# Graph network with two mixtures of experts: ranks by running counts, biases on VectorE, another order in the first router, five row buffers, small groups of tiles at both ends

## The chip, the cores and the metric

One Trainium2 chip, one of its cores. The kernel is one program; its metric is the time of an execution in microseconds (us) on the device, and a kernel's time is the median of its runs. TensorE (PE, with its weight loads PEld), VectorE (DVE), ScalarE (ACT), GpSimd (POOL) and SyncE (SP) run in parallel and wait for each other by semaphores. A granted clock of 1.0 is TensorE's upper level, 2.4 GHz, and 0.5 its lower one, 1.2 GHz.

## What is computed

A graph of N = 6250 nodes with 256 features and 106250 edges; four blocks, each added to x:

```python
x = x + gnn0(layernorm(x))      # two graph convolutions: relu(A (x W1) + b1), then A (h W2) + b2
x = x + moe0(layernorm(x))      # 6 experts, 2 of them per node
x = x + gnn1(layernorm(x))      # mish(x Wd^T + bd), messages over edges, mish(. Wo^T + bo)
x = x + moe1(layernorm(x))      # 8 experts, 2 of them per node

def moe0(f):                    # the router of block 2
    rh = relu(f @ router_w1 + router_b1)
    p = softmax(rh @ router_w2 + router_b2)
    top_w, top_i = top_k(p, 2)
    w = softmax(top_w)
    return sum_k w[k] * expert[top_i[k]](f)
```

The second mixture's router takes its two largest logits of `xn @ Wr + br` and their softmax. Each node's normalised row is written twice into a table ordered by expert; the row number there is the expert's region plus the node's rank among the nodes that chose that expert.

## The kernel before

x lies in SBUF the whole time as T = 52 tiles of 128 nodes (`c.x`), of which NT = 49 hold real ones. The program runs in stages with a barrier between them: setup, support (x W1), edge sums, `stage_hidden`, edge sums (which also make the second graph block's edge values), `stage_dispatch` with mix 0 (first router), `stage_experts`, `stage_nodes`, `stage_edges`, `stage_dispatch` with mix 1 (second router), `stage_experts`, `stage_last`.

`UNITS` cuts the 49 tiles into groups that routers, nodes and last stage take as their step: twelve of four tiles and one of one tile. Each engine has its own instruction list, written out by hand as calls of small functions of a unit u. The order of those calls is the order in the engine's queue, and an engine that waits holds back all that follows.

*Hidden layer* (`stage_hidden`): 13 rounds of two halves. ScalarE makes relu with the bias b1, TensorE transposes, VectorE copies to `rows` and frees the buffer that ScalarE waits for, SyncE stores.

*Router* (`stage_dispatch`), per unit: TensorE's `product` (the features of the edge stage times `wx`, plus the bias as one bf16 pass over three rows, which `split_bias` has made on VectorE out of the bias beforehand, line 1356); in the second router VectorE's `bounded` and ScalarE's `factor`; VectorE's `added` (to x, and the moments); ScalarE's `guessed`, VectorE's `refined` (1/deviation); ScalarE's `spread` (normalised rows into `xn`, a ring of RING = 4 buffers); TensorE's `turned` (transposes), ScalarE's `evacuated`; in the first router TensorE's `hidden` and ScalarE's `rectified`; TensorE's `logits`; VectorE's `biased`, in the first router ScalarE's `exponents`; VectorE's `chose` (the two largest, a matrix `chosen` of ones); TensorE's `ranks`; VectorE's `rows_of` (the row numbers); GpSimd's two scatters per tile (line 1340). A scatter waits for `row_ready`; `spread` waits until the buffer's scatters of four units before have landed; `product` waits until `added` has read the PSUM buffer (one in the first router, two in the second).

Before, `ranks` counts by matmuls: one with the matrix `before` (rows above in the same tile), n - 1 with `ones` for the earlier tiles, and n with `ones` for the total. An f32 matmul shows as two passes in the trace, so a unit of four tiles has 16.

TensorE's order before, in unit u: `turned(u)`, in the first router `hidden(u)`, then `ranks(u-1)`, `logits(u)`, `product(u+2+mix)`.

*Nodes* (`stage_nodes`): GpSimd gathers two expert rows per node (line 985), VectorE combines them into x, normalisation as in the router, a product with its bias pass (line 1119), ScalarE's four steps of `factor`, VectorE's `finished`, transposes back, ScalarE's `keep`. *Last stage*: gathers (line 689), two multiply-adds per tile, stores.

## Time and profile before

| | us |
|---|---|
| median of 3 runs | 5092.37 |
| lowest, highest | 5085.95, 5160.59 |
| profiled execution, its time | 5088.62 |
| its span | 5086.8 |
| TensorE busy | 3534.2 (69%) |
| GpSimd busy | 2862.7 (56%) |
| VectorE busy | 2214.1 (44%) |
| ScalarE busy | 1566.5 (31%) |
| mean granted clock | 0.744 |

The busy shares are means over stages that differ: in the experts TensorE is nearly full, in the edge stages GpSimd. What an edit in a router is worth is read in the router's own stretch: when each engine's part of a unit starts, and which wait ends last ahead of it. In a timeline row stand start, duration, engine, line, operation, output<-input, count, and in brackets how long the engine had stood idle and what released it. A name with q (PEq, DVEq) is an engine's sequencer.

### The profile page before, as it was taken

Reading aid. Unit: us, or ns where it says so; the run is one execution under the profiler, and the core shown is the slowest. Engines: PE = TensorE matmul, PEld = TensorE weight load, DVE = VectorE, ACT = ScalarE, POOL = GpSimd, SP = SyncE. Lnnn points to the kernel's source line nnn. Section 1 sums busy time; section 2 is a strip of 40 time slices with the busy share of each in tenths; the row PEclk is TensorE's granted clock in tenths of the full one; section 3 lists DMA queues with packets and bytes.
Section 4 is the critical chain, followed back from the end, with each engine's and each line's share of the span. In section 5 each row is a group of like instructions: output and inputs, shape, how many; then the busy total and the mean of one; then the engine's idle time right before and its main releaser. Section 6 shows DMA issues by size and latency. Waiting matters only on the chain. (4 is left out here: it accounts for less than half of the span.)

```text
span 5086.8 us, 59929 instructions
## 1 busy us (share of the span) xinstructions
PE 3534.2 (69%) x15835; PEld 3011.7 (59%) x15835; DVE 2214.1 (44%) x4333; ACT 1566.5 (31%) x1876; POOL 2862.7 (56%) x2934
## 2 busy tenths in 40 slices
PE   3677676775677777776779966666666667679980
PEld 2566565653565665664468745666666665568870
DVE  4555555554555555553423363333333334512113
ACT  1444444443444444442211153221112214311110
POOL 0777777774777777773500075777777772600007
PEclk9887878786878888885689975555555556689995
DMA  3555555553554554541232244666666661241214
GB/s 95 182 174 167 175 171 176 171 172 114 163 159 152 159 155 156 159 151 48 71 134 83 80 130 148 199 199 202 200 199 199 198 200 45 76 165 60 66 62 145
DMA packets 335855, 732.42 MB, mean 144 GB/s; under 512 B 67567, under 2 KB 184692, under 8 KB 335661
## 3 DMA queue, kind: packets, MB, share of 16 engines
q1 hardware_dynamic: 161244, 392.41, 22.5%
q0 software_dynamic: 117664, 283.67, 20.1%
q10 hardware_dynamic: 56880, 55.58, 3.3%
q8 instruction: 26, 0.43, 0.0%
q14 instruction: 41, 0.33, 0.0%
HBM read 520.48 MB, written 210.91 MB: 144 GB/s over the span
## 5 line engine op out<-in xcount | busy, mean ns | idle before, releaser
L593 PE MATMUL conv_pz<-conv_we,conv_edge 128*128 128x256 f32 x3360 | 1020.6, 471 | 23.7 <-PEq L73 23.7
L463 POOL DMA_INDIRECT conv_gath<-support_table,conv_idx x832 | 801.4, 963 | 390.2 <-issue 244.1
L1187 POOL DMA_INDIRECT x_node<-node_table,x_idx x840 | 849.6, 1011 | 296.2 <-issue 235.2
L1202 PE MATMUL x_pa<-x_hot,x_node 128*128 128x64 f32 x3360 | 765.7, 423 | 356.9 <-PEq L73 356.9
L463 POOL DMA_INDIRECT conv_gath<-hidden_table,conv_idx x832 | 803.4, 966 | 308.1 <-issue 247.1
L1202 PEld LDWEIGHTS x_pa<-x_hot,x_node 128*128 128x128 f32 x3360 | 732.4, 330 | 390.5 <-issue 390.5
L584 PE MATMUL conv_ps<-conv_hot,conv_gath 128*128 128x64 f32 x3328 | 531.4, 312 | 612.7 <-DMA conv_gath<-hidden_table,conv_idx 278.0
L593 PEld LDWEIGHTS conv_pz<-conv_we,conv_edge 128*128 128x128 f32 x3360 | 804.7, 246 | 172.8 <-issue 24.5
L584 PEld LDWEIGHTS conv_ps<-conv_hot,conv_gath 128*128 128x128 f32 x3328 | 485.3, 222 | 695.0 <-DMA conv_gath<-hidden_table,conv_idx 340.4
L897 ACT ACTIVATE conv_q<-conv_q 128x1024 f32<-128x1024 f32 x210 | 221.9, 1057 | 1106.2 <-ACTq L73 1064.1
L1223 DVE TENSOR_TENSOR x_node<-x_node,x_neg 128x1024 f32<-128x1024 f32 x210 | 257.4, 1226 | 624.3 <-DMA x_node<-node_table,x_idx 624.3
L1212 ACT ACTIVATE x_node<-x_node 128x1024 f32<-128x1024 f32 x210 | 221.9, 1057 | 896.6 <-ACTq L73 896.6
L689 POOL DMA_INDIRECT cb_outs<-expert_outs,row x98 | 96.4, 984 | 522.4 <-PEq L672 492.9
L480 DVE TENSOR_TENSOR conv_pz<-conv_pz,conv_bias 128x1024 f32<-128x1024 f32 x210 | 258.8, 1232 | 274.1 <-DVEq L73 268.2
L835 ACT ACTIVATE e_hid<-e_ph,e_b_first 128x256 f32<-128x256 f32 x344 | 137.8, 473 | 709.8 <-ACTq L73 709.8
L796 PE MATMUL e_ph<-e_xt,e_w_first 128*128 128x256 f32 x1376 | 313.4, 385 | 61.3 <-PEq L73 61.3
L497 DVE TENSOR_TENSOR sums_table<-sums_table,conv_ps 128x64 f32 x416 | 92.2, 222 | 596.3 <-DVEq L73 596.3
L1340 POOL DMA_INDIRECT expert_rows<-r_xn,r_row x196 | 198.3, 1012 | 264.2 <-DVE r_row L1559 210.7
L796 PEld LDWEIGHTS e_ph<-e_xt,e_w_first 128*128 128x128 f32 x1376 | 259.0, 192 | 106.3 <-issue 72.8
L985 POOL DMA_INDIRECT n_outs<-expert_outs,row x98 | 95.3, 972 | 402.5 <-POOLq L98 366.7
L481 DVE TENSOR_SCALAR conv_q<-conv_pz 128x1024 f32<-128x1024 f32 x210 | 257.1, 1224 | 31.8 <-DVEq L73 8.3
L873 DVE TENSOR_TENSOR e_outs<-e_py,e_b_last 128x512 f32<-128x512 f32 x114 | 78.8, 691 | 429.6 <-DVEq L73 429.6
(212 smaller groups left out, 4123.7 us busy)
## 6 DMA issues: line engine op xcount, KB each, us to landing
conv_edge<-in_edge_t SPq DMA_DIRECT2D x210, 512.0 KB, 5.1
edge_mish_table<-conv_neg SPq DMA_DIRECT2D x210, 512.0 KB, 3.0
x_neg<-edge_mish_table SPq DMA_DIRECT2D x210, 512.0 KB, 3.5
e_rows<-expert_rows SPq DMA_DIRECT2D x114, 256.0 KB, 3.1
expert_outs<-e_outs ACTq DMA_DIRECT2D x114, 256.0 KB, 2.2
expert_outs<-conv_zeros ACTq DMA_DIRECT2D x35, 512.0 KB
x_node<-node_table,x_idx POOLq DMA_INDIRECT x840, 3.1
conv_gath<-support_table,conv_idx POOLq DMA_INDIRECT x832
```

The costliest lines, as they stand in the source:

```text
L463: pool.indirect_dma_start(gath[s][:, j, :], None, table[:, :], bass.IndirectOffsetOnAxis(ap=idx[:, half, col:col + 1], axis=0),).then_inc( ...
L480: link(dve, nc.vector.tensor_tensor(ps_z[r][:], ps_z[r][:], bias[:].unsqueeze(1).to_broadcast([P, CG, D]), ALU.add), neg_own)
L481: nc.vector.tensor_scalar(q[r][:], ps_z[r][:], ZMAX, None, ALU.min).then_inc(z_ready[r], 1)
L584: last = pe.matmul(ps[s % 2][:], gath[s][:, j, :], hot[half][:, at + j, :], start=j == 0, stop=j == CG - 1)
L593: last = pe.matmul(ps_z[r][:, j, :], edge[r][:, m, j * P:(j + 1) * P], we[:, m, :], start=m == 0, stop=m == KD - 1)
L796: last = pe.matmul(out[:, m, :], w[:, k, m * P:(m + 1) * P], given[:, k, :], start=k == 0, stop=k == KD - 1)
L897: link(act, act.activation(q, q, ACT.Exp), own)
L1187: pool.indirect_dma_start(node[s][:, j, :], None, c.t3[:, :], bass.IndirectOffsetOnAxis(ap=idx[:, half, col:col + 1], axis=0),).then_inc(g ...
L1202: last = pe.matmul(ps_a[n][:, m, :], node[s][:, j, m * P:(m + 1) * P], hot[n][:, j, :], start=j == 0, stop=j == CG - 1)
L1212: act.activation(node[s][:], node[s][:], ACT.Relu, scale=-1.0).then_inc(msg_ready, 1)
L1223: nc.vector.tensor_tensor(node[s][:], node[s][:], neg[s % RING][:], ALU.add).then_inc(own, 1)
L1340: pool.indirect_dma_start(c.rows_d[:, :], bass.IndirectOffsetOnAxis(ap=row[0:rows, t + s, k:k + 1], axis=0), xn[u % RING][0:rows, s, :], None,
```

## The change

- `UNITS` has sizes 1, 3, ten times 4, 3, 1, 1: fifteen units instead of thirteen.
- Biases: `split_bias` and the bf16 pass go. In the nodes and in the second router VectorE adds the bias to the whole product in PSUM ahead of `bounded`. In the first router it is no longer there at all: `stage_hidden` adds it to x, 13 times 128x1024 elements.
- Ranks: `chose` ends with a multiply and a reduce that give each tile the count of the tiles before it (and the total as an extra slot), `sums`; `ranks` is then two matmuls, one with `ones` over `sums`, one with `before`: four passes.
- `logits(u-1)` stands in the first router behind `turned(u)`, then `product(u+2)`, `hidden(u)`, `ranks(u-1)`; ScalarE and VectorE are ordered to fit. The second router keeps its order.
- RING is 5 instead of 4.

```diff
-UNITS = tuple((t, min(TG, NT - t)) for t in range(0, NT, TG))
+SIZES = (1, 3) + (TG,) * 10 + (3, 1, 1)
+UNITS = tuple((sum(SIZES[:u]), n) for u, n in enumerate(SIZES))
@@ stage_hidden, VectorE, in each of 13 rounds
+                nodes = c.x[:, bass.ds(g * TG, TG), :]
+                nc.vector.tensor_tensor(nodes, nodes, b2[:].unsqueeze(1).to_broadcast([P, TG, D]), ALU.add)
@@ stage_nodes and the second router, VectorE, bounded(u); ps_x there
+                chain(nc.vector.tensor_tensor(ps_y[u % 2][:, 0:n, :], ps_y[u % 2][:, 0:n, :], bias[:].unsqueeze(1).to_broadcast([P, n, D]), ALU.add))
@@ product(u), routers; likewise in the nodes
-                        pe.matmul(ps_x[u % X][:, s, :], c.feat[:, k, (t + s) * P:(t + s + 1) * P], wx[:, k, :], start=k == 0, stop=False)
-                    last = pe.matmul(ps_x[u % X][:, s, :], ones3[:], parts[:], start=False, stop=True)
+                        last = pe.matmul(ps_x[u % X][:, s, :], c.feat[:, k, (t + s) * P:(t + s + 1) * P], wx[:, k, :], start=k == 0, stop=k == mix)
@@ ranks(u)
-                pe.matmul(flat(ps_r[:, 0:n, :]), before[:], flat(now[:, 0:n, :]), start=True, stop=n == 1)
-                for d in range(1, n):
-                    pe.matmul(flat(ps_r[:, d:n, :]), ones[:], flat(now[:, 0:n - d, :]), start=False, stop=d == n - 1)
-                for s in range(n):
-                    last = pe.matmul(ps_r[:, TG, :], ones[:], now[:, s, :], start=s == 0, stop=s == n - 1)
+                pe.matmul(flat(ps_r[:, 0:n + 1, :]), ones[:], flat(sums[u % 2][:, 0:n + 1, :]), start=True, stop=False)
+                pe.matmul(flat(ps_r[:, 0:n, :]), before[:], flat(chosen[u % 2][:, 0:n, :]), start=False, stop=True).then_inc(rank_ready, 1)
@@ chose(u), its end
+                slots = upto[:, 0:n + 1, :, 0:n]
+                taken = now.rearrange("p s e -> p e s").unsqueeze(1).to_broadcast([P, n + 1, 8, n])
+                chain(nc.vector.tensor_tensor(counted[:, 0:n + 1, :, 0:n], taken, slots, ALU.mult))
+                nc.vector.tensor_reduce(sums[u % 2][:, 0:n + 1, :], counted[:, 0:n + 1, :, 0:n], AX.X, ALU.add).then_inc(sums_ready, 1)
@@ TensorE, first router, for u in range(U)
+                    if u:
+                        logits(u - 1)
+                    if u + 2 < U:
+                        product(u + 2)
                     hidden(u)
+                    if u:
+                        ranks(u - 1)
@@ ScalarE, first router, for u in range(U)
                 evacuated(u)
                 if u + 1 < U:
                     spread(u + 1)
+                    if u:
+                        exponents(u - 1)
                     rectified(u)
+                    if u + 2 < U:
+                        guessed(u + 2)
@@ VectorE, first router, for u in range(U)
+                    if u >= 2:
+                        rows_of(u - 2)
+                    if u + 1 < U:
+                        refined(u + 1)
+                    if u:
+                        biased(u - 1)
                         chose(u - 1)
+                    if u + 2 < U:
+                        added(u + 2)
```

## Rows read from the trace of the kernel before

**Rows 1.** Stages: stretch, length, busy (count) of PE, PEld, DVE, ACT, POOL; clock; DMA share, GB/s.

```profile
1203.00:1245.00 42.00, 16.95 (x52) 7.58 (x52) 11.04 (x26) 13.10 (x26) 0.00 (x0) 0.50 0.27 81
...
2313.00:2552.00 239.00, 172.19 (x591) 103.28 (x591) 98.96 (x555) 56.09 (x116) 95.26 (x98) 0.59 0.16 56
...
2927.00:3103.00 176.00, 112.09 (x441) 79.71 (x441) 107.63 (x305) 108.18 (x154) 97.51 (x101) 0.73 0.39 117
...
4220.00:4449.00 229.00, 163.82 (x735) 120.83 (x735) 122.47 (x554) 102.63 (x155) 103.02 (x98) 0.67 0.17 58
...
4950.00:5087.00 137.00, 0.00 (x0) 0.00 (x0) 41.10 (x98) 0.00 (x0) 96.41 (x98) 0.50 0.47 140
```

**Rows 2.** First router's scatters: the line (ns; first to last start), then timeline.

```profile
L1340 POOL DMA_INDIRECT expert_rows<-r_xn,r_row x98: 954/960/1560, 2364.0 to 2536.0; - x98
...
2503.61 0.96 POOL L1340 DMA_INDIRECT expert_rows<-r_xn,r_row  x1 [7.78 <-DVE r_row L1559]
...
2552.07 0.59 POOL L775 DMA_DIRECT2D e_w_first<-in_m_w  x1 [14.52 <-POOLq L98]
```

**Rows 3.** Timeline, TensorE in one unit of the first router.

```profile
2383.51 1.97 PE L945 MATMUL r_pt<-ident_sb,r_xn 128*128 128x128 f32 x8
...
2386.58 3.78 PE L1371 MATMUL r_ph<-r_xt,r_w 128*128 128x512 f32 x4 [1.10 <-ACT r_xt L1436]
...
2390.15 0.44 PE L1394 MATMUL r_pr<-r_chosen,r_before 128*128 128x32 f32 x2
...
2392.05 1.06 PE L1379 MATMUL r_pl<-r_w,r_hid 128*128 128x6 f32 x8
...
2398.19 1.97 PE L945 MATMUL r_pt<-ident_sb,r_xn 128*128 128x128 f32 x8
```

**Rows 4.** Timeline, start of the first router, and ranks at the lower clock.

```profile
2319.81 0.28 DVE L880 CAST r_bias_high<-r_bias 3x256 bf16<-3x256 f32 x1 [4.91 <-DMA r_before<-in_before]
...
2325.09 1.19 PE L1355 MATMUL r_px<-r_wx,sums_table 128*128 128x256 f32 x2 [16.84 <-DVEq L1569]
...
2326.22 0.39 PE L1356 MATMUL r_px<-r_bias_parts,r_ones 3*128 3x256 bf16 x1
...
2326.54 1.22 PE L1355 MATMUL r_px<-r_wx,sums_table 128*128 128x256 f32 x2
...
2517.53 1.85 PE L1398 MATMUL r_pr<-r_chosen,r_ones 128*128 128x8 f32 x8
```

**Rows 5.** Second router: timeline around one product; scatters.

```profile
4341.21 1.22 DVE L1494 TENSOR_SCALAR r_q<-r_px 128x1024 f32<-128x1024 f32 x1 [3.51 <-PE r_px L1356]
...
4343.60 1.23 DVE L1506 TENSOR_TENSOR x_sb<-x_sb,r_q 128x1024 f32<-128x1024 f32 x1
...
4343.76 1.89 POOL L1340 DMA_INDIRECT expert_rows<-r_xn,r_row  x1 [0.30 <-issue]
...
4346.73 2.08 PE L1355 MATMUL r_px<-r_wx,messages_table 128*128 128x256 f32 x4 [1.05 <-DVE mv L914]
...
4354.86 1.22 DVE L1494 TENSOR_SCALAR r_q<-r_px 128x1024 f32<-128x1024 f32 x1 [3.52 <-PE r_px L1356]
...
L1340 POOL DMA_INDIRECT expert_rows<-r_xn,r_row x98: 954/960/1907, 4280.5 to 4432.3; - x98
...
4389.52 0.96 POOL L1340 DMA_INDIRECT expert_rows<-r_xn,r_row  x1 [2.91 <-DVE r_row L1559]
```

**Rows 6.** Timeline of the hidden layer, VectorE.

```profile
1213.15 0.42 DVE L663 COPY h_rows<-h_ps 128x256 f32<-128x256 f32 x1 [1.38 <-DVEq L73]
```

**Rows 7.** Timeline of the nodes, ScalarE and VectorE.

```profile
3062.97 2.08 ACT L937 ACTIVATE n_xn<-x_sb,n_shift,rstd 128x256 f32<-128x256 f32 x4 [1.73 <-DVE n_shift L931]
...
3071.59 1.22 DVE L1033 SCALAR_TENSOR_TENSOR n_rows<-n_q,n_py 128x1024 f32<-128x1024 f32 x1 [1.92 <-ACT n_q L1080]
```

**Rows 8.** Instructions by line: multiply of 32, reduce of 392 elements (busy us, mean ns).

```profile
L1554 DVE TENSOR_TENSOR r_picked<-r_is_nth,r_place 128x32 f32<-128x32 f32 (+1 forms) x52 | 7.5, 186 | 3.8
...
L1625 DVE TENSOR_REDUCE r_moved<-r_picked 128x49 f32<-128x392 f32 x4 | 2.1, 556 | 0.1
```

More of the change, by code:

```diff
@@ L658, in _ @@
             dve.sem_inc(rows_out[1], 16)
+            dve.wait_ge(b2_in, 16)
             with dve.Fori(0, G) as g:
@@ L960, in stage_nodes @@
         wd = sb("wd", [P, KD, D])
-        bias, parts, ones = bias_buffers(sb)
+        bias = sb("bias", [P, D])
         ln2 = sb("ln2", [P, 1])
@@ L1284, in stage_dispatch @@
             hid = sb("hid", [P, GN])
-            loads = [(wx[:, 0, :], "g_w2"), (bias[0][:], "g_b2"), (w1[:], "r0_w1"), (b1[:], "r0_b1"), (w2[:], "r0_w2")]
+            loads = [(wx[:, 0, :], "g_w2"), (w1[:], "r0_w1"), (b1[:], "r0_b1"), (w2[:], "r0_w2")]
         else:
@@ L1407, in _ @@
                 if mix == 0:
+                    if u:
+                        logits(u - 1)
+                    if u + 2 < U:
+                        product(u + 2)
                     hidden(u)
-                if u:
-                    ranks(u - 1)
-                logits(u)
-                if u + 2 + mix < U:
-                    product(u + 2 + mix)
+                    if u:
+                        ranks(u - 1)
+                else:
+                    if u:
+                        ranks(u - 1)
+                    logits(u)
+                    if u + 3 < U:
+                        product(u + 3)
+            if mix == 0:
+                logits(U - 1)
             ranks(U - 1)
@@ L1470, in _ @@
             spread(0)
+            if mix == 0:
+                guessed(1)
             for u in range(U):
-                if mix == 0 and u:
-                    exponents(u - 1)
                 evacuated(u)
@@ L1492, in bounded @@
                 n = UNITS[u][1]
+                got = ps_x[u % X][:, 0:n, :]
                 dve.wait_ge(px_ready, u + 1)
+                chain(nc.vector.tensor_tensor(got, got, bias[:].unsqueeze(1).to_broadcast([P, n, D]), ALU.add))
                 nc.vector.tensor_scalar(q[u % 2][:, 0:n, :], ps_x[u % X][:, 0:n, :], ZMAX, None, ALU.min).then_inc(z_ready, 1)
@@ L1549, in rows_of @@
                 dve.wait_ge(rank_ready, u + 1)
-                nc.vector.tensor_tensor(running[1 - u % 2][:], at_start[:], ps_r[:, TG, :], ALU.add)
+                nc.vector.tensor_tensor(running[1 - u % 2][:], at_start[:], ps_r[:, n, :], ALU.add)
                 chain(nc.vector.tensor_tensor(place[:, 0:n, :], ps_r[:, 0:n, :], at_start[:].unsqueeze(1).to_broadcast([P, n, 8]), ALU.add))
@@ L1562, in _ @@
                 nc.vector.memset(logit[r][:], -1e30)
-            nc.vector.memset(ones[:], 1.0)
-            nc.vector.memset(ones3[:], 1.0)
+            chain(nc.vector.memset(upto[:], 0.0))
+            for s in range(1, TG + 1):
+                nc.vector.memset(upto[:, s, :, 0:s], 1.0)
             if mix == 1:
                 nc.vector.memset(ln2[:], LN2)
+            nc.vector.memset(ones[:], 1.0).then_inc(consts_ready, 1)
             dve.wait_ge(w_in, 16 * len(loads))
-            split_bias(dve, nc, c, bias, parts, parts_own)
-            dve.sem_inc(parts_ready, 2)
             nc.vector.tensor_scalar(first[:], iota8[:], float(REGION), None, ALU.mult)
@@ L1576, in _ @@
             refined(0)
-            for u in range(U):
-                if u:
-                    biased(u - 1)
-                    if mix == 1:
-                        chose(u - 1)
-                if mix == 1 and u + 2 < U:
-                    bounded(u + 2)
-                if u + 1 < U:
-                    added(u + 1)
-                if u and mix == 0:
-                    chose(u - 1)
-                if u and mix == 1:
-                    rows_of(u - 1)
-                if u + 1 < U:
-                    refined(u + 1)
-                if u and mix == 0:
-                    rows_of(u - 1)
+            if mix == 0:
+                added(1)
+                for u in range(U):
+                    if u >= 2:
+                        rows_of(u - 2)
+                    if u + 1 < U:
+                        refined(u + 1)
+                    if u:
+                        biased(u - 1)
+                        chose(u - 1)
+                    if u + 2 < U:
+                        added(u + 2)
+                rows_of(U - 2)
+            else:
+                for u in range(U):
+                    if u:
+                        biased(u - 1)
+                        chose(u - 1)
+                    if u + 2 < U:
+                        bounded(u + 2)
+                    if u + 1 < U:
+                        added(u + 1)
+                    if u:
+                        rows_of(u - 1)
+                    if u + 1 < U:
+                        refined(u + 1)
             biased(U - 1)
```

67 lines of the change are left out of this document (25 added, 42 removed).

## The prediction

> **What bounds the kernel now.** I first cut the profile into its stages (busy time by stretch) [rows 1]. The edge stages and the experts are untouched. The change lies in five stretches: hidden layer 42 us, first router 239, nodes 176, second router 229, last stage 137. No engine is full in them, so each is read by its own timeline.
>
> Last stage: 98 gathers leave GpSimd one behind the other; 98 times 1.25 us fill it [rows 1]. Both routers end with GpSimd's 98 scatters, which need a row number first. In the first router a 4-tile unit is scattered in 8 times 1.27 = 10.1 us, yet nine units take (2503.61 - 2364.04) / 9 = 15.5 us each: GpSimd waits for the row numbers [rows 2]. TensorE sets that pace. In one unit it does transposes (2.0), waits for the copy of xt (1.1), runs the hidden layer (3.6), the ranks (16 passes, 1.9), the logits (0.9) and a product (about 5.3), with no other gap [rows 3], and its granted clock is 0.59 in the mean [rows 1], so mostly its lower level of 1.2 GHz.
>
> In the second router the pace is a ring of two engines: VectorE bounds a product, then adds the unit before it and takes its moments (4341.21 to 4346.7, 5.5 us) while TensorE waits 1.05 for the freed buffer; then TensorE's product takes 8.1 us while VectorE ends up waiting 3.52. Together 13.65 us a unit [rows 5]. In the nodes ScalarE sets the pace: VectorE waits for it (1.92) and it waits for VectorE only 1.73 [rows 7].
>
> **The change, part by part.**
>
> *Start of the routers.* TensorE now starts at 2325.09, after ten small VectorE steps that split the bias; the last load had landed by 2319.8 [rows 4]. With the split gone it starts some 5.4 us earlier; the memset of the new table lies under the loads.
>
> *First router, one unit.* Ranks fall from 16 passes to 4, at 0.23 each at the lower level (1.85 for eight [rows 4]): 0.9. The bias pass is 0.32 per tile, from 2326.22 to 2326.54, and leaves. A tile's two passes take 1.13 with it between them; 4 tiles so cost at most 4.5. I take 4.0, as passes of one kind should pack closer. The wait of 1.1 for the copy goes, because logits and product now stand between transposes and hidden layer. All at the lower level: 2.0 transposes + 1.7 logits (8 passes, twice 0.9 less overlap) + 4.0 + 3.4 hidden + 0.9 = 12.0 us. At the mean level of now (0.59 against 0.5) it is 10.2.
>
> VectorE has 99.0 us in 12.25 units, 8.1 a unit [rows 1]. The running counts add a multiply and a reduce of 160 elements: between 0.18 (32 elements) and 0.56 (392) each [rows 8], I take 0.3, so 8.7. GpSimd's 10.1 is then the floor. I take 10.7 for the round; bounds 10.1 and 12.0.
>
> *Small units at the start, first router.* From 2319.4: unit 0 (one tile) needs product 1.1, add and moments 1.1, deviation 2, transpose, hidden layer and logits, and waits in turn for products of units 1 and 2 and for ScalarE, which now does exponents after the spread; laid out by hand its rows are ready at 2344, those of unit 1 (three tiles) at 2354 and of unit 2 (tiles 4 to 7) at 2365. Now tiles 4 to 7 come at 2364.0 + 15.5 = 2379.5 or so. Then nine rounds of 10.7 and 18 scatters (units 11 to 14) of 1.27: 2365 + 96.3 + 22.8 = 2484. Now the last scatter starts at 2536.0 and ends at 2537.5, and the experts' first work follows 14.5 later [rows 2]. **-53.5**. Floor, 90 scatters in a row from 2365: 2479, -58.5. All at the lower level: 2496, -41.5.
>
> *Five row buffers.* A row group is held from its spread to its landed scatter; with the new order that is about 4.2 rounds, so four would stall and five just do. Nothing else.
>
> *Second router.* The ranks are not in the ring (TensorE waits anyway): nothing. In the ring the bias moves from TensorE to VectorE: + 1.22 (another pass over 128x1024, as the bounding [rows 5]); TensorE loses four bias passes of 0.2 to 0.3. The product's 16 passes take 7.2 us at the lower level (four take 2.08 [rows 5], each starting before the last has ended, so some 0.45 each) and about half at the upper. Round: 5.5 + 1.2 + 3.7 to 7.2 = 10.4 to 13.9. VectorE alone needs 13.65 - 3.5 + 1.2 + 0.65 = 12.0. Before each product TensorE will stand longer idle than now, so I expect it to begin at the lower level, as now: 13.4. The small first units and the earlier start bring tiles 4 to 7 to about 4292 (now 4280.5 + 13.6 = 4294.1). Six rounds of 13.4, one of 11.4 (a 3-tile product), then 34 scatters of 1.27 back to back, since the last products are small: 4427. Now the last 34 start at 4389.52 and the last of them at 4432.3, ending at 4433.9 [rows 5]. **-7** (round of 12.0: -15; of 13.9: -4).
>
> The Trainium skill, GPSIMD Engine Reference, Key points, says that GpSimd shares its SBUF interfaces with VectorE and is disturbed by VectorE instructions with two SBUF inputs. The trace agrees at one place: the scatter issued at 4343.76 took 1.89 us instead of 0.96 beside the addition at 4343.60, which reads two SBUF tiles [rows 5]. Its new case here is the running counts' multiply, 0.3 us; what it would make of the time is a rival below.
>
> *Nodes.* ScalarE's work per unit is unchanged. VectorE's extra 1.22 lies under its wait of 1.92 for ScalarE [rows 7], with little left over. Gain at the head: TensorE's first product is no longer in front of the next transposes as long, about -2. Loss at the tail: three small units cost one more ScalarE round (fixed latencies of some 4 us) than now, +4. **+2**, bounds -5 and +8 (half a us per round if the cover is too thin).
>
> *Hidden layer.* VectorE adds the bias to x 13 times, 1.23 us each. It idles 1.38 ahead of every other copy [rows 6], but some 0.6 of that passes before the addition can issue. So 1.23 + 0.6 - 1.38 = 0.45 late per round, times 13: **+6** (bounds +1, +14). The rounds are a ring through ScalarE, so a late copy delays all.
>
> *Last stage.* GpSimd stays full; its last unit was one tile already. **0**.
>
> Sum: -53.5 - 7 + 2 + 6 = -52.5. The profiled execution took 5088.6 (span 5086.8); its forecast is 5036. The median of the runs, 5092.4, lies 3.8 above it, so I forecast 5040.
>
> **Rivals.**
> (a) *TensorE keeps bounding the first router*, at its lower level throughout: 12.0 a round, -41.5 instead of -53.5: 5052. For it: 0.59 is near 0.5 now. Against: with 12 narrow rank passes and the bias passes gone, what is left is denser. 0.17.
> (b) *GpSimd is held up by VectorE.* If each first-router unit gets one scatter of 1.89, as the second has, the floor of a round is 11.1: 12 x 0.93 = 11 later: 5051. The added multiply is four times shorter than the addition that did it, which speaks against. 0.10. The page named above would have this one.
> (c) *The second router's product runs at the upper level*: 12.0 a round, 8 more: 5032. 0.15.
> (d) *Slower than before.* ScalarE's spread waits for a buffer's scatter, and behind it on ScalarE stand exponents and the hidden layer's rectifying, on which the row numbers hang. If five buffers close that ring, the first router's round becomes scatter + landing + rank chain, some 18 us: 9 x 7.3 = 66 more than forecast, 5106. It decides from a round of 16.5 on. Against: VectorE and TensorE need 9 to 12, and the hold time of 4.2 rounds leaves 0.8. 0.03.
> (e) *Far more than forecast*: would need scatters under 1.27 us; nothing shows it. 0.02.
> The forecast has 0.53.
>
> **From this to the numbers.** Two per cent is 102 us; about that is what a measurement of this kernel tells from no change. Every case but (d) and (e) lies inside it: floors in all stages together give -58.5 - 15 - 5 + 1 = -77.5. So faster by over 2% 0.02, slower 0.02, same 0.96. The range takes in (a) to (c) with the bounds of the hidden layer and the nodes: 5018 to 5068.
>
> **What would show it.** First router: scatters of 4-tile units 10.1 to 11 us apart, GpSimd's wait ahead of them under 1 us, TensorE starting about 2319.5. If the round is 12 with GpSimd waiting 2, it is (a); scatters of 1.9 us there, (b). Second router: VectorE's wait for the product of about 1.5 us, round near 13.4; GpSimd's wait there near 2.6. Hidden layer some 6 us longer; nodes alike within 5; last stage 137. The forecast is wrong if the first router's rounds stay over 12.5, or if a wait on scattered rows appears on ScalarE.

## The result, and the profile after

| | before | after |
|---|---|---|
| median of 20 runs, us | 5092.53 | 5081.49 |
| lowest, highest | 5082.59, 5160.59 | 5021.53, 5095.44 |
| profiled execution, time (span) | 5088.62 (5086.8) | 5025.71 (5023.9) |

The ratio is 0.9938, with a 95% interval of 0.9909 to 0.9967: within 2%, as forecast. Times the 5092.4 that the forecast started from it gives 5061, inside the range of 5018 to 5068; the median of the 20 runs, 5081.5, lies 13 above that range.

One fact is needed to read these numbers: the times of both kernels stand at two levels with a gap between. After: 7 runs at 5021.5 to 5028.1 and 13 at 5079.8 to 5095.4. Before: 18 at 5082.6 to 5095.3 and 2 at 5154.1 and 5160.6. At equal level the change brings 68 us (median of the lower ones 5092.26 to 5023.91) or 73 (5157.3 to 5084.8). The medians differ by 11 only, because the changed kernel is mostly at its upper level and the old one mostly at its lower. The profiles of both are of the lower level. These levels of time are not the two levels of TensorE's clock; the granted clock over a whole execution of after is 0.743 to 0.755, without a gap.

Stages after, as in [rows 1] (stretch, length, busy of PE, PEld, DVE, ACT, POOL, clock, DMA share, GB/s); hidden layer, first router, nodes, second router:

```profile
1203.00:1247.00 44.00, 16.94 (x52) 7.54 (x52) 25.90 (x39) 13.13 (x26) 0.00 (x0) 0.50 0.26 80
...
2318.00:2499.00 181.00, 102.86 (x414) 77.00 (x414) 110.65 (x619) 56.28 (x126) 95.65 (x99) 0.70 0.21 74
...
2874.00:3050.00 176.00, 96.86 (x392) 79.17 (x392) 121.98 (x323) 111.43 (x170) 97.27 (x101) 0.74 0.40 118
...
4163.00:4387.00 224.00, 128.45 (x566) 108.81 (x566) 150.05 (x635) 108.29 (x172) 101.37 (x101) 0.68 0.18 61
```

The first router is almost a quarter shorter, with GpSimd busy for the same 95 us: the time went out of its waits. Its timeline, GpSimd's first scatters of groups and TensorE in one round, answers to [rows 2, 3]:

```profile
2350.25 0.99 POOL L1323 DMA_INDIRECT expert_rows<-r_xn,r_row  x1 [41.35 <-DVE r_row L1556]
2359.46 0.96 POOL L1323 DMA_INDIRECT expert_rows<-r_xn,r_row  x1 [6.95 <-DVE r_row L1556]
2369.30 0.96 POOL L1323 DMA_INDIRECT expert_rows<-r_xn,r_row  x1 [2.55 <-DVE r_row L1556]
2438.84 0.96 POOL L1323 DMA_INDIRECT expert_rows<-r_xn,r_row  x1 [0.30 <-DVE r_row L1556]
...
2404.54 0.45 PE L1375 MATMUL r_pr<-r_sums,r_ones 128*128 128x40 f32 x2 [3.42 <-DVE r_sums L1541]
2408.53 3.49 PE L1338 MATMUL r_px<-r_wx,sums_table 128*128 128x256 f32 x8
2414.67 0.41 PE L1375 MATMUL r_pr<-r_sums,r_ones 128*128 128x40 f32 x2 [0.94 <-DVE r_sums L1541]
2417.65 1.99 PE L1338 MATMUL r_px<-r_wx,sums_table 128*128 128x256 f32 x8 [0.65 <-DVE mv L900]
```

Behind the first scatter of the third group (2.55) GpSimd never waits again: only 0.30 stands before a scatter, its own spacing. The round is 2414.67 - 2404.54 = 10.13 us, eight scatters, and TensorE waits inside it. The second router's ring, as in [rows 5]:

```profile
4279.46 1.23 DVE L1486 TENSOR_TENSOR r_px<-r_px,r_bias 128x1024 f32<-128x1024 f32 x1 [1.97 <-PE r_px L1338]
4283.50 1.68 POOL L1323 DMA_INDIRECT expert_rows<-r_xn,r_row  x1 [0.30 <-issue]
4286.25 6.72 PE L1338 MATMUL r_px<-r_wx,messages_table 128*128 128x256 f32 x16 [2.46 <-DVE mv L900]
4288.08 0.96 POOL L1323 DMA_INDIRECT expert_rows<-r_xn,r_row  x1 [2.91 <-DVE r_row L1556]
4293.00 1.23 DVE L1486 TENSOR_TENSOR r_px<-r_px,r_bias 128x1024 f32<-128x1024 f32 x1 [2.08 <-PE r_px L1338]
```

Each wait has shifted the way that was forecast: VectorE's from 3.51 to 2.0, TensorE's from 1.05 to 2.46, the round from 13.65 to 13.5.

### The profile page after: what moved, and what is told of

Same layout as the page of the kernel before. It is cut to its first block and busy times, and to the rows that moved or that the text cites. A ratio compares the mean times of both kernels' runs of the same rounds, so it can differ in the third digit from the quotient of the medians.

```text
span 5023.9 us, 59359 instructions
## 1 busy us (share of the span) xinstructions
PE 3400.9 (68%) x15424; PEld 2955.7 (59%) x15424; DVE 2278.9 (45%) x4507; ACT 1575.5 (31%) x1918; POOL 2863.6 (57%) x2934
## 5 line engine op out<-in xcount | busy, mean ns | idle before, releaser
L1170 POOL DMA_INDIRECT x_node<-node_table,x_idx x840 | 851.3, 1013 | 289.2 <-issue 234.8
L584 PE MATMUL conv_ps<-conv_hot,conv_gath 128*128 128x64 f32 x3328 | 515.7, 305 | 623.8 <-DMA conv_gath<-hidden_table,conv_idx 295.3
L584 PEld LDWEIGHTS conv_ps<-conv_hot,conv_gath 128*128 128x128 f32 x3328 | 469.4, 216 | 707.5 <-DMA conv_gath<-hidden_table,conv_idx 352.5
```

The costliest lines, as they stand in the source:

```text
L584: last = pe.matmul(ps[s % 2][:], gath[s][:, j, :], hot[half][:, at + j, :], start=j == 0, stop=j == CG - 1)
L1170: pool.indirect_dma_start(node[s][:, j, :], None, c.t3[:, :], bass.IndirectOffsetOnAxis(ap=idx[:, half, col:col + 1], axis=0),).then_inc(g ...
```

## The experiments

Stage lengths below are differences of starts in the timelines, in us. First router: last gather of the second convolution to the experts' first weight load. Second router: last gather of the edge stage to the same. Nodes: first gather there to first of the edge stage. Edges: first to last gather. Kernels of one set ran together on one chip; the record numbers it 14 in sets 1 and 3 and 7 in sets 2 and 4, and gives no number for set 0.

| kernel | set | runs: median (lowest to highest) | first router | nodes | edges | second router |
|---|---|---|---|---|---|---|
| before | 0 | 5092.5 (5082.6 to 5160.6) | 249.5 | 171.7 | 1104.3 | 245.0 |
| after | 0 | 5081.5 (5021.5 to 5095.4) | 190.9 | 171.4 | 1105.9 | 232.3 |
| e1_same | 1 | 5068.3 (5062.6 to 5074.8) | 189.6 | 173.3 | 1153.3 | 235.4 |
| e2_units | 1 | 5016.0 (5013.9 to 5018.4) | 187.7 | 170.8 | 1104.4 | 235.4 |
| e3_ranks | 1 | 5023.8 (5022.0 to 5026.2) | 187.6 | 172.7 | 1105.0 | 234.3 |
| e4_order | 1 | 5096.2 (5062.7 to 5115.7) | 233.4 | 172.1 | 1117.8 | 235.2 |
| e5_order_only | 2 | 5038.7 (5034.7 to 5093.3) | 206.0 | 170.2 | 1103.1 | 247.0 |
| e6_split | 2 | 4991.1 (4987.2 to 4991.8) | 190.3 | 172.7 | 1070.6 | 234.2 |
| e7_noadd | 2 | 5006.5, one run | 190.7 | 173.3 | 1089.3 | 233.9 |
| e8_before_split | 2 | 5058.8 (5051.1 to 5067.3) | 255.0 | 170.5 | 1070.8 | 245.6 |
| e9_ring4 | 3 | 6331.1 (6316.8 to 6341.5) | 238.1 | 209.4 | 1496.6 | 242.3 |
| e11_ranks_units | 3 | 6329.9 (6291.8 to 6333.4) | 238.0 | 209.6 | 1505.8 | 239.9 |
| e10_before_units | 3 | 6181.4 (6165.4 to 6205.1) | 271.7 | 203.3 | 1322.2 | 261.0 |
| e12_all | 4 | 4978.6 (4975.3 to 4982.9) | 186.4 | 170.2 | 1069.9 | 235.1 |

Beside them the kernel before took 5087.7 in set 1, 5087.9 in 2, 6177.5 in 3 and 5092.8 in 4 (medians).

### Where the two levels are: e1_same

> The changed kernel again, nothing altered. Its executions stand at two levels, 5022 to 5028 us and 5080 to 5095 us, with nothing between; the profile on hand is of the lower one (5025.7). Theory A, one stage: in an execution of the upper level one stage is some 60 us longer and all others are as profiled, so a profile of that level shows one stretch 60 us longer with another granted clock. Theory B, everywhere: the two convolution stages and the edge stage (3240 us together, paced by the gathers that GpSimd issues) each take some 1.8 per cent more. Theory C, the routers' gain is lost again: at the upper level the first router's scatters leave every 15 us as before (54 us more). A profile of the lower level again would tell nothing between them, except that it repeats: scatters of 4-tile units 10.13 us apart in the first router, 13.4 in the second.

All five runs, 5062.6 to 5074.8, lie far above the lower level of 5022 to 5028, and the profiled one is 42.7 us longer than the profiled run of after. It is theory A in that one stage is longer, but not in its size (47 us, not 60) and not by another clock. The line of the gathers in the edge stage, which the change does not touch, from after and from e1_same (ns smallest/median/largest; first to last start; then busy us, mean ns, idle):

```profile
L1170 POOL DMA_INDIRECT x_node<-node_table,x_idx x840: 942/946/1994, 3047.2 to 4153.1; - x168
L1170 POOL DMA_INDIRECT x_node<-node_table,x_idx x840 | 851.3, 1013 | 289.2 <-issue 234.8 <-POOLq L74 54.3
```

```profile
L1170 POOL DMA_INDIRECT x_node<-node_table,x_idx x840: 942/946/1860, 3039.1 to 4192.4; - x168
L1170 POOL DMA_INDIRECT x_node<-node_table,x_idx x840 | 898.7, 1070 | 289.7 <-issue 234.9 <-POOLq L74 54.9
```

The mean gather takes 57 ns more, times 840 = 48 us, and the stage is 47.4 longer; GpSimd's idle time is the same to 0.5 us. So the instructions themselves are stretched. The granted clock of the stage is 0.50 in both: TensorE's clock is not the cause. In set 0 the upper level lay higher, 61 us above the lower one (5084.8 and 5023.9), and none of its runs was profiled: where the other 13 or so went is not shown. The timelines around VectorE's addition of the edge values, after first, then e1_same:

```profile
3603.58 0.95 POOL L1170 DMA_INDIRECT x_node<-node_table,x_idx  x1 [0.30 <-issue]
3603.75 1.23 DVE L1206 TENSOR_TENSOR x_node<-x_node,x_neg 128x1024 f32<-128x1024 f32 x1 [2.93 <-DMA x_node<-node_table,x_idx]
3604.84 0.96 POOL L1170 DMA_INDIRECT x_node<-node_table,x_idx  x1 [0.31 <-issue]
...
3609.27 1.23 DVE L1206 TENSOR_TENSOR x_node<-x_node,x_neg 128x1024 f32<-128x1024 f32 x1 [3.08 <-DMA x_node<-node_table,x_idx]
3609.85 1.45 POOL L1170 DMA_INDIRECT x_node<-node_table,x_idx  x1 [0.30 <-issue]
```

```profile
3601.02 1.23 DVE L1206 TENSOR_TENSOR x_node<-x_node,x_neg 128x1024 f32<-128x1024 f32 x1 [3.34 <-DMA x_node<-node_table,x_idx]
3601.70 1.37 POOL L1170 DMA_INDIRECT x_node<-node_table,x_idx  x1 [0.30 <-issue]
...
3606.57 1.23 DVE L1206 TENSOR_TENSOR x_node<-x_node,x_neg 128x1024 f32<-128x1024 f32 x1 [3.18 <-DMA x_node<-node_table,x_idx]
3607.13 1.49 POOL L1170 DMA_INDIRECT x_node<-node_table,x_idx  x1 [0.30 <-issue]
...
3612.68 1.55 POOL L1170 DMA_INDIRECT x_node<-node_table,x_idx  x1 [0.30 <-issue]
```

A gather that starts while the addition runs is longer than 0.95 by what is left of the addition, less 0.13: at 3609.85 the addition has 0.65 left and the gather takes 0.50 more. For the 155 (after) and 207 (e1_same) gathers stretched by an addition, what is left less the stretch lies between 0.115 and 0.145. Gathers start every 1.25 us, so nearly every addition meets one; what counts is when. After: 209 gathers start during an addition, 0.39 us before its end in the mean, stretch 54 us in all; e1_same: 207, 0.63 us, 105 us. At the lower level the offsets from gather to addition alternate (0.12, 0.65, 0.11, 0.70: every other addition costs nothing), at the upper they stand near 0.65 each time. Both patterns repeat themselves. A likely reason, not tested, is that each addition waits for the landing of its gathers (3.18 us in the rows), so that a delayed gather shifts the next addition too. A gather that had started before the addition is never stretched, not even by 0.1 us (203 such gathers in after, 207 in e1_same). Stretch per 100 us of the edge stage, added up from the gathers:

```
before    6.9 5.0 4.8 5.0 4.8 5.0 5.3 5.0 5.2 4.8 5.5
after     6.7 5.4 5.1 4.6 4.9 5.1 5.1 4.8 5.1 4.8 6.2
e1_same   8.8 9.4 9.3 8.8 9.4 8.7 9.5 9.1 9.7 9.4 9.7
e4_order  8.9 9.4 9.6 5.2 5.0 5.6 4.9 5.4 4.9 5.3 4.9
```

e4_order changes over after 300 us; its profiled run took 5081.2, between its levels of 5062.7 to 5069.8 and 5111.2 to 5115.7.

### Which part brings the routers' gain: e2_units, e3_ranks, e4_order, e5_order_only

```diff
e2_units: after, with
-SIZES = (1, 3) + (TG,) * 10 + (3, 1, 1)
+UNITS = tuple((t, min(TG, NT - t)) for t in range(0, NT, TG))
```

> The changed kernel with the old groups: twelve of four tiles and one of one tile. If GpSimd's issue is the floor of the first router (10.13 us for eight scatters, back to back), what the small groups bring is the earlier first scatter: now it starts at 2350.25 and GpSimd has 9.5 us of holes until the third group. With a four-tile group first its rows come some 33 us after the first product (2325.5), at 2358 to 2362, and 98 scatters of 1.27 follow: the first router ends 4 to 8 us later. In the second router the first rows come some 48 us after its first product instead of 34, and the last groups no longer end in small products: 5 to 10 us later. Nodes 4 us shorter (two rounds less). Lower level of the time 5030 to 5040. Rival: the groups do nothing in the first router because something else is the floor: then it ends within 2 us of now and the lower level stays at 5022 to 5028.

Neither the expected cost nor the rival came: the first router is 2 to 3 us shorter with the old groups (the time, 5016, is below both forecasts), the second as in e1_same. The first scatter leaves 5.8 to 6.5 us later after the first product (30.5 against 24.7 and 24.0), but then GpSimd has no holes at all, and 98 scatters back to back end earlier.

```diff
e3_ranks: after, with
-                pe.matmul(flat(ps_r[:, 0:n + 1, :]), ones[:], flat(sums[u % 2][:, 0:n + 1, :]), start=True, stop=False)
+                (before's 16 passes; no multiply and reduce in chose)
```

> The changed kernel with the ranks counted by 16 matmul passes per group of four again, without VectorE's multiply and reduce. TensorE gets 12 passes back, 0.11 to 0.23 us each: 1.3 to 2.8 us a round, against 0.9 to 4.2 us that it waits per round now. Theory A: TensorE has room, GpSimd's issue stays the floor, round 10.1 to 10.7, first router 0 to 5 us longer, lower level of the time 5023 to 5031. Theory B: the running counts were what brought the round down: 12 us or more, first router 18 us longer or more, 5044 or more. Second router alike within 3 us under both.

Theory A, even below its range of 0 to 5 us more: 187.6, 2 to 3 us shorter, as with the old groups.

```diff
e4_order: after, with TensorE's
-                    logits(u - 1); product(u + 2); hidden(u); ranks(u - 1)
+                hidden(u); ranks(u - 1); logits(u); product(u + 2)      (and ScalarE, VectorE to fit)
```

> The changed kernel with the order of steps of the kernel before in the first router (TensorE: transposes, hidden layer, ranks, logits, product; ScalarE and VectorE to fit); ranks, biases, groups and ring as changed. Theory A, the order carries the gain: TensorE waits 1.1 us for the copy again and again stands between rows and product; of the old 15.5 us only 12 rank passes (1.4 to 2.8) and four bias passes (1.2) are gone: round 11.5 to 13, first router 13 to 29 us longer, lower level of the time 5037 to 5055. Theory B, fewer passes carry it: the round stays near 10.1 and the time within 3 us of 5025.

Theory A, and beyond its range: 43 us longer, the round 14.71. TensorE in that round:

```profile
2411.42 1.98 PE L1353 MATMUL r_ph<-r_xt,r_w 128*128 128x512 f32 x4 [1.10 <-ACT r_xt L1413]
2415.09 0.41 PE L1375 MATMUL r_pr<-r_sums,r_ones 128*128 128x40 f32 x2 [1.69 <-DVE r_sums L1527]
2418.63 1.87 PE L1361 MATMUL r_pl<-r_w,r_hid 128*128 128x6 f32 x8 [2.91 <-ACT r_hid L1425]
```

With fewer passes in the old order, TensorE stands 1.10 + 1.69 + 2.91 = 5.7 us. The round falls from 15.5 to 14.7 only: what the passes give back is lost again in waits for ScalarE and VectorE. Over the whole router, from TensorE's first product to its last pass, its busy time is 50 us less than before (122.3 for 172.2), its idle time 42 more (68.4 for 26.5).

```diff
e5_order_only: before, with after's order in the first router and RING = 5
```

> The kernel before with only the first router's new order of steps and five row buffers; 16-pass ranks, bias passes, split bias and the old groups stay. Read before this run: taking the new order out of the changed kernel made the first router 43 us longer (233.4 instead of 190, last gather to first weight load of the experts), taking the running counts out made it no longer (187.6). Theory A, the order is nearly all of it: round 10.1 to 11, first router 249.5 - 40 to 50 = 200 to 210 us, second router and hidden layer as before (245, 34), time 5035 to 5050 (85 to 100 if the edge stage is at its upper level). Theory B, the order works only together with fewer passes: round 12 or more, first router over 218 us, time 5058 or more.

Theory A at its lower end: 206.0, 43.5 us less than before, with all bias passes and 16-pass ranks still there. GpSimd waits for row numbers beyond its 0.30 only twice after the first scatter (1.19 and 4.14). Order and ring together, not told apart by any run, are so most of the gain; what is left to the biases is 206.0 - 186.4 (e12_all) = 19.6, of which 5.4 at the start.

How they brought it shows in TensorE. Its 591 passes are those of before, yet they keep it busy for 136.2 us in place of 172.2, at a granted clock of 0.70 for 0.59; its idle time falls from 26.5 to 12.7. Some 36 us of TensorE's 50 are so the same passes at a higher clock, and only 14 are waits. The router, then three stretches of it, by the columns of [rows 1]:

```profile
2310.00:2502.00 192.00, 136.15 (x591) 87.59 (x591) 96.84 (x550) 54.81 (x116) 95.33 (x98) 0.70 0.20 69
...
2380.00:2390.00 10.00, 10.00 (x34) 7.06 (x33) 5.37 (x26) 1.21 (x4) 6.75 (x8) 0.50 0.29 105
2390.00:2400.00 10.00, 10.00 (x23) 4.93 (x23) 5.13 (x27) 2.97 (x6) 7.68 (x8) 0.52 0.26 93
2400.00:2410.00 10.00, 10.00 (x62) 7.10 (x60) 5.90 (x38) 4.96 (x10) 4.76 (x5) 1.00 0.19 68
```

TensorE's hidden layer in four rounds, with GpSimd's longest wait:

```profile
2381.04 3.78 PE L1371 MATMUL r_ph<-r_xt,r_w 128*128 128x512 f32 x4
2397.06 3.23 PE L1371 MATMUL r_ph<-r_xt,r_w 128*128 128x512 f32 x4
2404.02 0.95 POOL L1340 DMA_INDIRECT expert_rows<-r_xn,r_row  x1 [4.14 <-DVE r_row L1573]
2406.90 1.98 PE L1371 MATMUL r_ph<-r_xt,r_w 128*128 128x512 f32 x4
2415.48 1.98 PE L1371 MATMUL r_ph<-r_xt,r_w 128*128 128x512 f32 x4
```

With every pass kept and TensorE never idle, the round from 2381.04 takes it 16.0 us at the lower clock, the one from 2406.90 takes 8.6 at the upper; GpSimd's floor is 10.1. GpSimd's two waits (1.19 and 4.14) come within and right behind this stretch at the lower clock. With the passes kept, the order reaches the floor only while the clock is up, and the clock fell to 0.5 here although TensorE was full.

### What the stretch is made of: e6_split, e8_before_split, e7_noadd

```diff
e6_split: after; e8_before_split: before; both with, in the edge stage
-                nc.vector.tensor_tensor(node[s][:], node[s][:], neg[s % RING][:], ALU.add).then_inc(own, 1)
+                for j in range(CG):
+                    last = nc.vector.tensor_tensor(node[s][:, j, :], node[s][:, j, :], neg[s % RING][:, j, :], ALU.add)
+                last.then_inc(own, 1)
```

> The changed kernel, and in the untouched edge stage VectorE's addition of two SBUF tiles (128x1024, 1.23 us, 210 times) cut into four of 128x256 (0.42 us each). Read before this run: at the lower level 176 of the stage's 840 gathers take more than 0.945 us and the stretch sums to 58.7 us (first to last gather 1105.9 us); at the upper one the stretch is 106.3 us (1153.3 us). A gather that starts during the addition lasts as much longer as is left of the addition, less some 0.13 us. Theory A, the port is held per instruction: after the cut a gather waits only for the short instruction it meets: at most 0.3 us, about 0.1 in the mean, some 1.3 times per group: 15 to 35 us of stretch in all, first to last gather 1060 to 1085 us, the two levels gone, time 4980 to 5005 us in every execution. Theory B, VectorE's total time counts: four instructions take 1.7 us in place of 1.23, the stretch stays at 59 or more, stage 1105 to 1160 us, time 5020 to 5075.

> The kernel before, with the same cut of the edge stage's addition into four. Theory A of the run above: first to last gather of the edge stage 1060 to 1085 us instead of 1104, time 5040 to 5065, no second level. The difference to the changed kernel with the same cut is then what the change itself brings, without the edge stage's two levels: by the stages read so far 58 (first router) + 10 (second) - 2 (hidden layer) = 60 to 66 us. Theory B: 5085 to 5140.

Theory A in both: edges 1070.6 and 1070.8, stretch 23.3 and 23.7 us, largest gather 1.2 us, and no second level shows (4 runs within 5 us, 10 within 16; for the kernel before, at its upper level in 8 of 60, ten runs without it prove little). Between the two kernels with the cut lie 5058.8 - 4991.1 = 67.7 us: that is what the change brings, somewhat over the 60 to 66 added up from the stages. e6_split against the kernel before: 0.979 (0.9735 to 0.9845), so faster, but whether by 2% is open.

```diff
e7_noadd: after, with (the messages lack the edge part)
-                nc.vector.tensor_tensor(node[s][:], node[s][:], neg[s % RING][:], ALU.add).then_inc(own, 1)
+                nc.vector.tensor_scalar(node[s][:], node[s][:], 1.0, None, ALU.mult).then_inc(own, 1)
```

> The changed kernel, and in the edge stage the addition of the edge values is left out: in its place VectorE multiplies the gathered tile by 1 (one SBUF input, same tile, same waits, so the messages lack the edge part). Theory A, two SBUF inputs on VectorE hold GpSimd up: all 840 gathers take 0.94 to 0.95 us, stretch near 0, first to last gather 1045 to 1055 us, time 4965 to 4975. Rival: any VectorE instruction that touches SBUF does it, or the DMA queue: stretched gathers stay, stage over 1080 us.

The rival is right: a multiply with one input stretches gathers too (41.9 us, edges 1089.3), and is stretched itself. The pattern is another one, though. The 133 gathers that start during a multiply are longer by what is left of it less 0.13 us, as with the addition (17 us in all). But here gathers that started before the multiply are caught too (another 17 us): one that would end sooner ends 0.12 us after the multiply. A multiply that starts later in a gather waits in its place, 0.89 instead of 0.69 us. The last 7 us fall to gathers that meet no multiply. First such a waiting multiply, then a caught gather:

```profile
3601.45 0.89 DVE L1206 TENSOR_SCALAR x_node<-x_node 128x1024 f32<-128x1024 f32 x1 [3.13 <-DMA x_node<-node_table,x_idx]
3605.96 1.31 POOL L1170 DMA_INDIRECT x_node<-node_table,x_idx  x1 [0.30 <-issue]
3606.46 0.69 DVE L1206 TENSOR_SCALAR x_node<-x_node 128x1024 f32<-128x1024 f32 x1 [3.02 <-DMA x_node<-node_table,x_idx]
```

Its 0.69 us is near half of the addition's 1.23. But it is not any VectorE instruction: in the second convolution of after 302 gathers start during 1.2 us instructions that read PSUM (lines 480, 481, 488), with no stretch at all, while 54 that start during the one-hot comparison out of SBUF (line 506) are stretched by 13.2 us in sum. The Trainium skill, SBUF — State Buffer, Who interferes with whom, says that the two engines share one pair of SBUF ports as an exclusive lock for a whole instruction, that a VectorE instruction in the fast two-port mode takes them, and that one with at most one SBUF input outside that mode, as those that read PSUM are, does not. The traces agree. It also infers that an addition of two SBUF inputs would not hold up GpSimd's making of DMA descriptors; for these gathers the measurement decides against it (105 us in e1_same). They also read their offsets from SBUF, and no run tells whether that is the part held up.

### Where the kernel before took 6178 us: e9_ring4, e11_ranks_units, e10_before_units

```diff
e9_ring4: e6_split with RING = 4.  e11_ranks_units: e6_split with old groups and ranks.  e10_before_units: before with new SIZES.
```

> The changed kernel with the edge stage's addition cut into four (the kernel of the run before that stood at 4987 to 4992 us, first router 190.3 us), and four row buffers instead of five. Theory A, by the hold time: a buffer is held from its spread to its landed scatters for 4.2 rounds of 10.1 us, so with four ScalarE waits for the landed scatters ahead of a spread, and the round grows to 10.5: first router 193 to 197 us, time 4990 to 4998. Rival: the wait on ScalarE holds back exponents and rectifying behind it as well, and the round becomes scatters + landing + chain, over 12 us: first router over 207 us, time over 5004. Third: four are enough, nothing moves (under 1 us).

> The changed kernel with the addition cut into four, the old groups of four and the old 16-pass ranks: what is left of the change is the new order, five buffers and the biases off TensorE. Read before: old groups alone 187.7 us for the first router, old ranks alone 187.6, both as changed 190.3; the order alone on the kernel before 206.0 (its first product 5.1 later, its first scatter 8.9 later after that, and 4.4 of holes). Theory A, counts and small groups bring nothing beside the other parts: first router 184 to 190 us, second 233 to 237, time 4978 to 4990. Theory B, each covers for the other: with both gone first scatters come late and holes open as in the kernel with the order alone: first router 194 to 201 us, time 4992 or more.

> The kernel before with only the new groups (1, 3, ten times 4, 3, 1, 1), in routers, nodes and last stage. It asks what puts the edge stage at its upper level (every addition meets a starting gather 0.6 us before its end, stretch 9.4 us per 100) or its lower (every other one, 5.0). Theory A, the new groups at the end of the nodes do: upper level in more than half of the executions, as in the changed kernel (the kernel before: 6 of 53). Theory B, they do not: a quarter or less. The stages themselves: first router 240 to 252 us (249.5 to 255 now), second 240 to 246 (245), lower level of the time 5075 to 5092, upper 5125 to 5145.

None of these was answered: the kernel before took 6177.5 here, although the record gives the number of the chip as 14, as in set 1, where it took 5087.7. What differed is not known. Engines fall silent for long with nothing to wait for that the profile shows. e9_ring4, edge stage, TensorE's last product and VectorE after it:

```profile
4185.89 3.65 PE L1185 MATMUL x_pa<-x_hot,x_node 128*128 128x64 f32 x16 [3.52 <-issue]
...
4183.14 1.42 DVE L1207 TENSOR_TENSOR x_node<-x_node,x_neg 128x256 f32<-128x256 f32 x4
4203.28 0.29 DVE L1216 TENSOR_TENSOR messages_table<-messages_table,x_pa 128x128 f32 x1 [18.71 <-DVEq L74]
```

The product was done at 4189.5, VectorE adds it at 4203.3. Such a hole comes once in each pass of VectorE's loop, and behind it GpSimd's starts lie 13.5 to 14.2 us apart instead of 1.25 (32 such gaps in 1424 us). With the addition in one piece, in e10_before_units, these gaps are 4.8 to 8.4. So the kernels with the cut, 18 more instructions in the loop, take 174 to 184 us more in the edge stage here (1322.2 to 1496.6 and 1505.8). They differ from e10_before_units in the routers too, but elsewhere that left the edge stage alike (1070.6 and 1070.8). e9_ring4 is slower than the kernel before by 1.0252 (1.0224 to 1.0279); e11_ranks_units is slower as well, 1.0231 (1.0197 to 1.0264), its 2% just unclear. That VectorE's own instructions arrive late is what it looks like; no run tests it. One row of e9_ring4 still serves, ScalarE's waits in the first router (us in total, times, longest):

```profile
ACT r_xn L923 <- DMA expert_rows<-r_xn,r_row: 13.4, 5, 5.2
```

With four buffers ScalarE does wait for scattered rows; with five no such row stands there in e11_ranks_units, nor in after. What four would cost in the other sets stays open, and so does whether the new groups favour the upper level.

### Everything useful together: e12_all

```diff
e12_all: e6_split with old groups, old ranks, and in the convolutions
-                link(dve, nc.vector.tensor_tensor(hot[half][:], c.iota[:]..., part_of(rel), ALU.is_equal), own)
+                for b in range(0, HALF_COLS, CG): ... (128x256 each; the same for the multiply by c.weight)
```

> A chip apart: the three runs before this one ran where the kernel before took 6178 us instead of 5088 (its gather stages 1463, 1444 and 1322 us instead of 1059, 1056 and 1104), so they told nothing on holes of a few us. Here the changed kernel with old groups, old 16-pass ranks, the edge stage's addition in four, and in both convolution stages each of the two SBUF-only passes that make the one-hot matrices (128x768, 0.95 us) in three of 128x256. The three sit in separate stages. Groups and ranks, theory A (they bring nothing beside order, buffers and biases): first router 184 to 190 us, second 233 to 237; theory B (each covers for the other): first router 194 to 201. One-hot passes: of the convolution's 832 gathers only those that start during these passes are stretched (44 of 103 gave 14 us in one stage, 51 of them 15 us in the other; those that start during an addition out of PSUM not at all), so 5 to 10 us less in each stage, 1046 to 1053 instead of 1053 to 1059, if the gathers pace the stage, nothing if TensorE does. Edge stage 1070 as in the run with the cut alone. Time 4965 to 4985 us if both hold, on a chip where the kernel before takes 5088.

First router 186.4, second 235.1: theory A. Counts and groups bring nothing beside order, buffers and biases. The convolutions take 1054.7 and 1052.1 us, for 1056.3 to 1059.4 and 1053.0 to 1058.8 in the other kernels outside set 3: cutting the one-hot passes is worth some 3 us each at most, not the 5 to 10 expected. 4978.6 us, 0.9766 (0.9699 to 0.9833) of the kernel before: faster, though not surely by 2%, and the fastest version found, with the reserve that kernels with the cut additions lost under the conditions of set 3.

## Why the prediction was right and where it was wrong

By stage, forecast and measured (profile after less profile before, both at the lower level):

| | forecast | measured |
|---|---|---|
| first router | -53.5 | -58.6 |
| second router | -7 | -12.7 |
| nodes | +2 | -0.3 (e6_split less e8_before_split: +2.2) |
| hidden layer | +6 | +2.2 (last gather to first gather, 55.8 to 58.0) |
| last stage | 0 | +0.7 |
| stages not touched | 0 | +5.8 |
| sum | -52.5 | -62.9 |

*Start of the routers.* Right: 22.5 us from the last gather to the first product became 17.6, 4.9 less for 5.4.

*First router.* GpSimd's issue was the floor, as said, and the round mis-sized: 10.13, the floor itself, where 10.7 was taken to be careful; 9 rounds times 0.57 = 5.1 is the difference. The three first groups' rows came 24.7, 34 and 43.8 after the first product, for 24.6, 34.6 and 45.6 by hand.

*Why it reached the floor.* Here the number came out for reasons that the sum did not price, and that was in part luck. The prediction added up TensorE's passes, counted the new order as the 1.1 us wait for the copy alone, and took the clock of now, 0.59, to stay. By that sum the order without the shorter ranks would have left a round of 15.5 - 1.1 = 14.4. e5_order_only took 10.1 in most rounds, since its passes ran at a higher clock (0.70 over the router) and TensorE waited less. e4_order shows the other half: the passes gone are worth 0.8 us a round without the new order, since TensorE then waits longer for ScalarE and VectorE. What raises the clock was not tested; no run holds it fixed. That the shorter ranks bring nothing (e3_ranks) holds at the clock that these runs had.

*Rival (a)*, TensorE at its lower level throughout, did not come: its granted clock rose from 0.59 to 0.70 in the mean, and of the products in the rows above one ran in 3.49 us and the next in 1.99. Its price was too high as well: at the lower clock TensorE goes from the ranks at 2404.54 to the hidden layer at 2411.85, 7.3 us, and with 3.6 for a hidden layer at that clock (e5_order_only) an estimate of the round is 10.9, where the sum had 12.0.

*Second router.* The round is as forecast (13.45 in the mean of four, for 13.4), VectorE waits 2.0 for 1.5, GpSimd 2.91 for 2.6. The surplus of 5.7 is in the head: the group of tiles 4 to 7 comes 5.9 us earlier than before, not 2.1, and the first two rounds from there are 11.9 and 12.8. In these two the product ran in 5.1 and 6.0 us, in the others in 6.4 to 6.8: *rival (c)*, the product at the upper clock throughout, did not come, but a part of it did.

*Nodes, hidden layer, last stage.* Inside their bounds. In the hidden layer the addition lies almost wholly in idle time: 0.2 a round for 0.45.

*Rival (b)*, GpSimd held up by VectorE, was the right mechanism at the wrong place. In the first router no scatter is stretched but one (1.12 us) and the last two (1.56, as before). In the second one is in most rounds (1.43 to 1.83). But in the edge stage the mechanism decides over 47 us, between after and e1_same. *Rival (d)*: no wait on scattered rows appears on ScalarE.

*What failed* for the time is the last step, "The median of the runs, 5092.4, lies 3.8 above it, so I forecast 5040". It took the runs to scatter closely about the profiled one. They do not: 5040 falls into the gap between 5028 and 5080, where no execution of the changed kernel lies, and that the ratio of all runs (5061) falls into the range is no merit of the sum but a mixture of two levels. For the lower level alone the profile shows 62.9 us gained for 52.5. The table of before had 5160.59 as one of three runs, 68 us above the median, and the prediction never asked where it came from. It took "the edge stages and the experts are untouched" to mean that they keep their time. They keep their code; but whether VectorE's additions fall into the cheap or the dear pattern is settled anew in each execution. The changed kernel fell into the dear one in 13 of 20 and 5 of 5 runs, the kernel before in 8 of 60 outside set 3 (where the text of e10_before_units says 6 of 53, it was 7), e2_units and e3_ranks in none of 4 each, e5_order_only in 1 of 10, e4_order in 5 of 10 and in one more for a part of the stage. Why the changed kernel does so more often is open: new groups are common to those with many, but e3_ranks has them too.

## What to carry to other kernels

When the runs of a kernel show a value far from the others, find the stage that it comes from before forecasting a change: a median between two levels can hide six times what it shows. Where GpSimd issues DMAs back to back, look for VectorE instructions that work on SBUF alone, and compare a gather's mean with its median: 1013 and 1070 ns over a median of 946 was the whole story. Before pricing passes that leave an engine, ask what it would wait for without them; in the first router the order of steps with a fifth row buffer was worth 43.5 us and the shorter ranks nothing. And where an engine's clock moves, compare its busy time for the same passes: the order saved more by faster passes than by waits.

## What the runs showed of the hardware

- A gather that starts during a VectorE addition with two SBUF inputs is longer by the rest of that instruction less 0.13 us; one that started before the addition is not stretched (203 gathers in after). A fast multiply with one SBUF input (0.69 us) also stretches gathers that started before it, or is stretched itself (up to 0.95 us, e7_noadd). Four additions of 0.42 us in place of one of 1.23 cut the stretch from 59 (or 106) to 23 us. Instructions of the same length that read PSUM stretch nothing (302 gathers).
- This coupling has two patterns that repeat themselves for hundreds of us, 5.0 and 9.4 us of stretch per 100, and an execution can change from one to the other midway (e4_order).
- The same 591 TensorE passes of the first router took 172.2 us at a mean granted clock of 0.59 and 136.2 at 0.70, in another order; within e5_order_only a full round took 16.0 us at the lower clock and 8.6 at the upper.
- One set of five ran the same kernel in 6178 instead of 5088 us, with the experts alike (377.7 and 502.3 us) and the loops of gathers up to 40% longer, holes of 5 to 20 us once per pass of a loop. There two kernels with 18 more short instructions in the loop were 2.3 and 2.5% slower than the kernel before, where like ones gained 2% in other sets. The cause is not known, nor whether it lies in the chip.
